# Masked attention of a Perceiver decoder: half of the softmax weights turned by VectorE blocks and device memory, weighing one place later, values copied by ScalarE

## The reference, cut to what matters

```python
Q = query @ Wq.T + bq ; K = key @ Wk.T + bk ; V = value @ Wv.T + bv      # 16 heads of 16
energy = einsum('bhqd,bhkd->bhqk', Q, K) / sqrt(16)
energy = where(mask == 0, -1e20, energy)
attention = softmax(energy, axis=-1)                                      # over 256 keys
x = einsum('bhqk,bhkd->bhqd', attention, V).reshape(b, -1, 256)
x = x @ Wo.T + bo
```

## Time and profile before

| | |
|---|---|
| median of three runs | 1993.7 us (1990.88 to 1994.27) |
| the profiled execution | 1994.13 us |
| its span | 1992.4 us |
| share of the span: PE, DVE, ACT, POOL | 98%, 62%, 56%, 30% |
| granted clock of TensorE | 0.996 |
| the 32 places of the masked attention | 981.4 to about 1250 us of the span |

### The profile page before, as it was taken

One profiled execution on the slowest core, in us unless ns is written; L12 is line 12 of the kernel. 1 busy time (PEld: TensorE's weight loads), 2 busy tenths in 40 slices (PEclk: granted clock), 3 DMA queues, 4 the chain that ended last, 5 costly groups with the idle time before them and its releaser, 6 DMA issues.

```text
span 1992.4 us, 43991 instructions
## 1 busy us (share of the span) xinstructions
PE 1944.6 (98%) x17307; PEld 1694.8 (85%) x17307; DVE 1231.6 (62%) x3579; ACT 1112.7 (56%) x2432; POOL 600.5 (30%) x652
## 2 busy tenths in 40 slices
PE   6999999999999998998999999999999999999998
PEld 5898998989998984777688887889999999999998
DVE  6767677776767665676588988438748623243212
ACT  5666666666667663332587877544444444444443
POOL 3111141111211101233122211444444444444444
PEclk9999999999999999999999999999999999999999
DMA  5556454555545441000311110001010010101000
GB/s 195 176 173 208 150 164 155 157 166 156 158 147 171 137 130 49 1 1 1 92 34 34 34 33 24 22 1 64 1 43 10 34 43 1 43 1 43 1 12 32
DMA packets 100332, 154.21 MB, mean 77 GB/s; under 512 B 12896, under 2 KB 78752, under 8 KB 100000
## 3 DMA queue, kind: packets, MB, share of 16 engines
q1 hardware_dynamic: 100128, 151.41, 24.4%
HBM read 103.73 MB, written 43.45 MB: 74 GB/s over the span
## 4 chain that ended last, share of the span: by engine, by line
PE 46%; ACT 2%; DVE 2%; issue 1%; POOL 0%; POOLq 0%; DVEq 0%; ACTq 0%
PE bank L83 21%; PE bank L1132 18%; PE bank L1053 2%; PE bank L1068 1%; PE bank L1040 1%; ACT att_p L1238 1%; PE bank L1098 1%; PE bank L1009 1%; ACT att_pt L1243 1%; PE bank L1079 0%; DVE dec_room L140 0%; POOL right_h L963 0%; ACT att_kt L1230 0%; PE bank L1091 0%; DVE att_vz L1385 0%
## 5 line engine op out<-in xcount | busy, mean ns | idle before, releaser
L963 POOL TENSOR_TENSOR right_h<-right_hr,right_h 128x512 fp32r<-128x512 f32 x256 | 341.7, 1335 | 417.6 <-ACT right_hr L1285 417.6
L1284 ACT ACTIVATE right_h<-bank,dec_b 128x512 fp32r<-128x512 f32 x256 | 176.2, 688 | 389.7 <-PE bank L83 368.0
L83 PE MATMUL bank<-lat_kv_t,lat_qk 128*128 128x320 f32 x1536 | 253.8, 314 | 1.7 <-DVE lat_qk L2456 1.7
L83 PE MATMUL bank<-lat_wv,lat_kv_t 128*128 128x512 f32 x960 | 243.3, 394 | 4.1 <-DVE lat_qk L2456 4.1
L83 PEld LDWEIGHTS bank<-lat_kv_t,lat_qk 128*128 128x128 f32 x1536 | 228.0, 188 | 14.6 <-DVE lat_qk L2456 5.3
L2320 ACT ACTIVATE lat_p<-bank,lat_neg_max 128x320 f32<-128x320 f32 x256 | 134.7, 527 | 146.5 <-DVE lat_neg_max L2461 146.5
L83 PEld LDWEIGHTS bank<-lat_wv,lat_kv_t 128*128 128x128 f32 x960 | 175.7, 189 | 34.9 <-DVE lat_qk L2456 4.5
L83 PE MATMUL bank<-dec_xt,dec_lo 128*128 128x512 f32 x512 | 200.5, 392 | 0.0
L2461 DVE TENSOR_REDUCE lat_neg_max<-bank 128x1 f32<-128x320 f32 x256 | 122.5, 485 | 95.3 <-PE bank L83 89.3
L1285 ACT ACTIVATE right_hr<-bank,dec_b 128x512 f32<-128x512 f32 x256 | 174.5, 682 | 0.0
L1132 PE MATMUL bank<-dec_hi,right_h 128*128 128x256 f32 x1024 | 161.6, 279 | 1.2 <-POOL right_h L963 1.2
(11 more groups left out here) (332 smaller groups left out, 3804.9 us busy)
## 6 DMA issues: line engine op xcount, KB each, us to landing
lat_turns<-lat_pb SPq DMA_DIRECT2D x63, 640.0 KB, 3.0
lat_pt<-lat_turns SPq DMA_DIRECT2D x252, 160.0 KB, 3.2
raw_w<-in_L_ffn_W SPq DMA_DIRECT2D x16, 1024.0 KB, 6.6
lat_ctx_raw<-in_ctx SPq DMA_DIRECT2D x16, 512.0 KB, 5.2
right_ctx_raw<-in_ctx_turned SPq DMA_DIRECT2D x16, 512.0 KB, 3.8
lat_kv_f<-in_ctx_turned SPq DMA_DIRECT2D x15, 512.0 KB, 4.4
lat_ctx_raw<-gate_rows SPq DMA_DIRECT2D x15, 512.0 KB, 4.8
lat_kv_t<-lat_lt SPq DMA_DIRECT2D x32, 128.0 KB, 4.5
```

What stands on the lines that cost most here:

```text
L83: mm = pe.matmul(out, lhs(a, k), rhs(b, k), start=first and k == 0 and n == 0, stop=last and k == KD - 1 and n == 2)
L963: pool.tensor_tensor(h[:, g % 2, 1, :], hr[:, g % 2, :], h[:, g % 2, 0, :].bitcast(F32), ALU.subtract).then_inc(h_lo, 1)
L1284: act.activation(h[:, n % 2, 0, :], h_bank[n % 2][:, :], ACT.Relu, bias=bias).then_inc(h_hi, 1)
```

## The change

1. Half m = 0 of places 0 to 30 is no longer turned by PE and ACT. DVE turns it in 32x32 blocks (`turn`, one transpose of 128x1024 from `p[0]` into `pb`), SP writes `pb` to device memory (`turns`, two buffers) and reads it back in four DMAs into `pt_early` (one buffer). `p[0]` now lies in place of the scores of that half (`sc[:, 0]`). Half m = 1, and both halves of place 31, are turned as before.
2. `weigh(b-1)` does both halves in one, as the last of PE's slot b, behind values_proj(b+1) and the side step. It waits for both ways of turning.
3. `normalise(b-1)` moves to the end of DVE's slot, behind `slot_late`.
4. The values are copied to `vz` (now three buffers) by ACT, without bias, out of `pt_bank[0]` (but for place 0). The bias of the values goes through `Wo` once: `output_bias` adds bv @ Wo to bo, as the weights of a row sum to one.
5. `project_output` moves ahead of keys_proj, into odd slots; side steps wait for the turn of the place before.
6. At the start, ACT's values_proj(0) stands ahead of its queries(0); it waits for POOL's fill of `vz`.

```diff
-            p = att.sb("p", [P, KD, R, S2])
-            pt = att.sb("pt", [P, KD, R, 2, P])
+            p_late = att.sb("p", [P, R, S2])
+            p = (sc[:, 0], p_late)
+            pb = att.sb("pb", [P, 4, R * 2, 32])
+            pt_early, pt_late = att.sb("pt_early", [P, 4, R, 2, 32]), att.sb("pt_late", [P, R, 2, P])
+            turns = nc.dram_tensor("att_turns", (2, P, R * S2), F32, kind="Internal").ap()
...
+            def weights_turned(b):                      # SP
+                sp.wait_ge(p_turned, b + 1)
+                wait(sp, pt_in[b % 2], 64 * (b // 2))
+                sp.dma_start(turns[b % 2], pb[:, :, :, :].rearrange("p g u c -> p (g u c)")).then_inc(p_out, 16)
+                sp.wait_ge(p_out, 16 * (b + 1))
+                wait(sp, o_psum, b)
+                for g in range(4):
+                    sp.dma_start(pt_early[g * 32:(g + 1) * 32].rearrange("p q r t c -> p q (r t c)"),
+                                 turns[b % 2].rearrange("(q p) (g c) -> g p q c", q=4, g=4)[g]).then_inc(pt_in[b % 2], 16)
...
-            for i in range(2, NT):
-                context(i)
+            context(2)
+            for b in range(B - 1):
+                weights_turned(b)
+                if b % 2 == 1 and (b + 5) // 2 < NT:
+                    context((b + 5) // 2)
...
             for b in range(B):                          # PE
                 energies(b)
+                if b == 0:
+                    output_bias()
                 if b >= 1:
                     turn(b - 1, 1)
+                if b >= 3 and b % 2 == 1:
+                    project_output((b - 3) // 2)
                 if b + 1 < B:
                     keys_proj(b + 1)
-                if b >= 1:
-                    weigh(b - 1, 0)
-                    weigh(b - 1, 1)
-                turn(b, 0)
-                if b + 1 < B:
                     values_proj(b + 1)
                 if b in in_slot:
-                    pe.wait_ge(pt_done, 4 * b + 2)
+                    pe.wait_ge(pt_done, 2 * b)
                     side_step(*in_slot[b])
-                if b >= 2 and b % 2 == 0:
-                    project_output(b // 2 - 1)
+                if b >= 1:
+                    weigh(b - 1)
             pe.wait_ge(s_low, 8 * B)
             hidden(0, 0)
+            turn(B - 1, 0)
             turn(B - 1, 1)
-            weigh(B - 1, 0)
-            weigh(B - 1, 1)
+            weigh(B - 1)
...
+            values_proj(0)                              # ACT, ahead of queries(0)
...
-                turn(b, 0)                              # ACT
                 for r in range(R):
+                    if b + 1 < B and r == 2:
+                        values_proj(b + 1)
                     weights_of(b, 1, r)
...
+            def turn(b):                                # DVE
+                dve.wait_ge(p_ready, 8 * b + 4)
+                wait(dve, p_out, 16 * b)
+                dve.transpose(pb[:, :, :, :], p[0].rearrange("p r (t g c) -> p g (r t) c", g=4, c=32)).then_inc(p_turned, 1)
...
             for b in range(B):                          # DVE
                 slot_head(b)
+                lowest(b, 0, 0, R)
                 if b >= 3 and b % 2 == 1:
                     residual(b // 2 - 1)
-                lowest(b, 0, 0, R)
                 lowest(b, 1, 0, R)
...
                 if b % 2 == 1:
                     add_bias(b // 2)
+                if b < B - 1:
+                    turn(b)
+                slot_early(b)
+                slot_late(b)
                 if b >= 1:
                     normalise(b - 1)
-                slot_early(b)
-                if b + 1 < B:
-                    values_proj(b + 1)
-                slot_late(b)
```

More of the change, by code:

```diff
@@ L890, in _ @@
                 sp.dma_start(mask_i[half * S:(half + 1) * S, :], w["mask_1x1xSxS2_ik1"]).then_inc(loads, 16)
-            for t in range(2):
-                sp.dma_start(bv[:, t, :], everywhere(w["L1_xattn_bv"])).then_inc(loads, 16)
+            with nc.allow_non_contiguous_dma(reason="a bias as a column"):
+                sp.dma_start(bv[:, :], column(w["L1_xattn_bv"])).then_inc(loads, 16)
             sp.dma_start(bo[:, :], everywhere(w["L1_xattn_bo"])).then_inc(loads, 16)
@@ L1236, in weights_of, with values_proj @@
                 if m == 1 and r == 0 and b >= 1:
[L1237 to L1238 removed]
+                    act.wait_ge(pt_psum, 2 * b)
+                act.activation(p[m][:, r, :], sc[:, m, r, :], ACT.Exp, bias=low[:, m, r:r + 1], scale=-1.0).then_inc(p_ready, 1)
             def turn(b, m):
+                u = turn_of(b, m)
                 for half in range(2):
[L1242 to L1244 removed]
+                    act.wait_ge(pt_psum, 2 * u + half + 1)
+                    own_r = slice(2 * half, 2 * half + 2)
+                    if m == 0:
+                        for n in range(2):
+                            ins = act.copy(pt_early[:, :, 2 * half + n, :, :],
+                                           pt_bank[half][:, n * 2 * P:(n + 1) * 2 * P].rearrange("p (t q c) -> p q t c", q=4, c=32))
+                        ins.then_inc(pt_done, 1)
+                    else:
+                        act.copy(pt_late[:, own_r].rearrange("p r t n -> p (r t n)"), pt_bank[half][:, :]).then_inc(pt_done, 1)
+            def values_proj(b):
+                act.wait_ge(v_psum, b + 1)
+                wait(act, o_psum, b - 2)
+                to = vz[:, b % 3].rearrange("p t m r e -> p (t m r e)").rearrange("p (u e) -> p u e", e=2 * W32)
+                src = values_bank(b)[:, :].rearrange("p (u h e) -> p u h e", h=2, e=HD)
+                for par in range(2):
+                    at = par * W32
+                    ins = act.copy(to[:, :, at:at + HD], src[:, :, par, :])
+                ins.then_inc(v_done, 1)
             def side_read(kind, c, j):
```

114 lines of the change are left out of this document (66 added, 48 removed).

## The result

| | kernel before | changed kernel |
|---|---|---|
| median | 1994.17 us (5 runs, 1990.88 to 1994.92) | 2002.61 us (5 runs, 2001.17 to 2006.62) |
| the profiled execution, its span | 1994.13, 1992.4 us | 2001.17, 1999.4 us |
| granted clock over the span | 0.996 | 0.993 |

The ratio is 1.0047, with a 95% interval of 1.0035 to 1.0059: the change makes the kernel slower by 0.47%. The prediction was 2000.5 us and slower, and its mechanism for the first ten places is the one that the trace shows. Two executions in the comparisons of this document, one of e3 and one of the kernel before beside c3, were slow ones at a low granted clock, and the ratios leave them out.

A forecast was written before the change was run, and what follows sets the result against it. PE was taken to bound the early places, with DVE nearly as full from place 10. Head +1.6, early +3.3, places 10 to 24 0, 25 to 30 -0.5, end +2.3 made +6.7: 2000.5 us, range 1987 to 2013.

The forecast's parts named there:

- the case itself: Whole kernel: the forecast of 2000.5 us, its own range 1998 to 2006, chance 0.42.
- The head: Start: PE's queries(1) comes later because ACT copies the values ahead of queries(0): +1.6 us, bounds 0 and +2.2.
- DVE's block turn: DVE, each place: transpose of 128x1024 takes 1.24 us, bounds 0.85 and 1.35; two early places 13.4 us, above PE's 12.82.
- The way: Block turn's end to last read's landing, through device memory: L = 7.6 us, bounds 6.7 and 8.6.
- The loop: Early places: normalise, lowest, turn, way and weighing hold two slots at 15.1 us; with filling the path, +3.3, bounds 0 and +7.
- Places 10 to 24: Later attention places, 130.46 us before: DVE's gain and the waits together 0, bounds -5 and +5.
- -5.1 and +5.1: Places 10 to 24: DVE's work if it never waits, -5.1 us, against waits of +1.3 and +3.8.
- three waits: Places 10 to 24, DVE: for the gates in slot 13, +1.3 us; for the experts' rows in slots 23 and 24, +3.8.
- Places 25 to 30: Six places like 17 to 22, DVE bound: -0.1 us each, -0.5 us.
- the charge of 3.8 us: Slots 23 and 24: normalise queues behind DVE's wait for ACT's copy of the experts' rows: +3.8 us for the two.
- The last place: Place 31: weigh(30) uncovered, turns before weigh(31); energies(31) to hidden(0, 1) 12.9 us against 10.53: +2.3, bounds +0.5 and +4.
- The values on ACT: ACT's copies, two places: 12.13 to 11.7 us, under PE's 12.82, so no term.

The follow-up runs named there:

- e3: Changed kernel with ACT's values_proj(0) behind queries(1) in the head: 1998.35 us, ratio 1.0028 to the kernel before.
- c3: Changed kernel with weighing behind the next place's energies, normalise, residual and project_output moved, two read buffers, queries first: 1990.74 us, ratio 0.9990 to the kernel before.
- e1: Changed kernel, weighing takes both halves from the one PE turned, so PE waits for no transfer; turn and transfers still run: 1991.86 us, ratio 0.9985.
- e4: Changed kernel with the early half written to device memory twice ahead of the reads: 2053.83 us, ratio 1.0302 to the kernel before.
- e8: As e1, with DVE's block turn and the transfers left out too: 1976.96 us, ratio 0.9915 to the kernel before.
- e9: Changed kernel with DVE's normalise ahead of the side work in places 23, 24 and 31: 2001.09 us, ratio 1.0048 to the kernel before.
- e2: Changed kernel with two buffers instead of one for the blocks read back: 2001.99 us, ratio 1.0038 to the kernel before.
- e11: Changed kernel with project_output behind keys_proj and residual behind lowest(b, 1): 1998.36 us, ratio 1.0026 to the kernel before.
- e6: Kernel before with only the values copied by ACT and their bias put through Wo once: 1993.11 us, ratio 0.9994 to the kernel before.
- e5: Changed kernel with PE's values_proj repeated, twice in place 1 and three times in place 3: 2003.39 us, ratio 1.0048 to the kernel before.
- c1: Changed kernel with two read buffers, queries first, values_proj repeated in places 1 and 3, project_output behind keys_proj: 1996.90 us, ratio 1.0019 to the kernel before.

## Why the prediction was right

Predicted 2000.5 (1998 to 2006 for the case itself), measured 2002.61: a growth of 6.8 us said, 8.4 found. The way through device memory in a loop that PE and DVE wait for is shown (e1, e4). That the number came so near is in part luck: the stage's terms were +1.6, +3.3, 0, -0.5 and +2.3, and the profiled execution has +1.6, +6.7, -2.4, +1.7 and +1.8, with -2.4 in stages that the change doesn't touch. Step by step:

**The head (+1.6).** As predicted: 20.49 against 18.9. ACT copies the values and only then the queries; PE's next query product waits for those:

```profile
965.85 0.65 ACT L1305 COPY att_vz<-bank 128x256 f32<-128x256 f32 x2 [4.42 <-PE bank L83]
966.38 1.46 ACT L1267 ACTIVATE q_bd<-bank,att_q_bias,att_q_scale 128x512 f32<-128x512 f32 x2
...
967.99 3.67 PE L1035 MATMUL bank<-rows_a,right_wq 128*128 128x512 f32 x8 [1.36 <-ACT q_bd L1267]
```

e3 undoes it.

**DVE's block turn (1.24 us).** All 31 in a view by tile (min, median, max in ns), the straight line through two smaller tiles was enough. What the step made of it was wrong: without the wait for the transfers two places take 13.11 us with DVE's turns (e1) and without them (e8), PE busy throughout, and not 13.4 with DVE as the bound.

```profile
L1446 DVE STREAM_TRANSPOSE att_pb<-att_sc x31: 1234/1237/1246, 986.2 to 1242.1; 128x1024 f32<-128x1024 f32 x31
```

**The way (L = 7.6 us).** 7.2 at its shortest (places 0 and 5), 7.7 on average over places 4 to 9, and 9.3 in place 2, beyond the upper bound of 8.6. e1 shows by its 10.8 us that it isn't hidden. The bound of 8.6 itself doesn't come out of the earlier trace rows: with their largest landing of the group, 3.8, the sum is 8.1. By the rule of the Trainium skill, "DMA: Bandwidth & Descriptors", section "Anatomy of one DMA", the way was 6.8, and the early places as fast as before. No place of the profiled execution came in that short.

**The loop (15.1 us for two places).** The steady part has it: energies(4) to (10) at 1014.14, 1030.12, 1045.36, 1060.20, so 15.98, 15.24, 14.84 us, 15.4 on average (the last is as short as two places were before). In place 6 DVE goes from normalise through `lowest` and split_keys to the block turn without standing still, and the way and the weighing follow, as the loop has it. Energies(2) was put at 996.5, and is at 996.47, which is luck: the turn ended 0.4 us and the way took 0.4 us less than said, and the weighing took 1.9 us in place of 1.1, at a granted clock of 0.50. What failed is the term's size: +3.3 predicted, +3.1 in e9's execution and +6.7 in the profiled one. The rest is what the first four places lose (32.9 us against 29.6 in e9) when a transfer comes late, as here (SP's queue, then the landings of all writes of the stage):

```profile
1003.02 0.34 SPq L937 DMA_DIRECT2D att_turns<-att_pb  x1
1007.86 2.12 SPq L941 DMA_DIRECT2D att_pt_early<-att_turns  x4
...
1014.31 1.73 SPq L941 DMA_DIRECT2D att_pt_early<-att_turns  x4
```

```profile
DMA to landing us min/median/max: 2.6/2.8/5.7
```

The reads at 1007.86 wait 4.8 us behind the write instead of 2.8, and those at 1014.31 for the weighing of place 2, which the same lateness had put off until then (the buffer is single). I had written that the single buffer adds nothing; in such a place it does, in the median of e2 it doesn't. The step's upper bound was too low by its own terms: with L at 8.6 they give +8, not +7.

**Places 10 to 24 (0).** -2.4 in the profiled execution, -0.9 in e9's, 0.0 in e3's. DVE is the fullest engine, as I said (118.7 of 128.0 us), though not without waits, and e8 and e4 both move the stretch: DVE's turn with the transfers, and the length of the way. That -5.1 and +5.1 cancelled was luck. The text names three waits and prices two, and neither of the two is seen in its place: place 13 takes 8.8 us (8.9 before), 23 and 24 together 16.8 (16.7). A wait that I hadn't priced is there instead, project_output's, 6.4 us in five places (e11).

**Places 25 to 30 (-0.5).** +1.7, the step that was wrong in sign. I had the charge of 3.8 us for the experts' rows in places 23 and 24, that is ahead of energies(25). A part of it falls in place 25, because PE must wait too: its turn's second bank is the one that DVE reads last.

```profile
1190.81 0.69 DVE L1561 TENSOR_TENSOR dec_xt<-bank,dec_xt 128x512 fp32r<-128x512 f32 x1 [0.95 <-ACT dec_xt L1322]
```

```profile
1191.65 0.63 PE L1086 MATMUL bank<-ident,att_p 128*128 128x128 f32 x4 [1.69 <-DVE dec_xt L1561]
1192.88 2.08 PE L1125 MATMUL bank<-att_wo,att_ot 128*128 128x256 f32 x4 [0.61 <-DVE att_ot L1474]
```

DVE's wait for ACT, 0.81 before, is 0.95; behind it PE waits 1.69 and then 0.61 for the normalised rows. Energies(25) to (26) is 12.1 us, 9.0 before. Place 27 grew more, 12.2 against 8.5, and place 29 has 11.5 against 9.8, with the experts' rows in neither: in place 27 PE waits 1.50 us for DVE's addition of the cell's result to x (L1553) and 1.39 for the normalised rows. Behind the waits of places 25 and 27 the granted clock is 0.50, as the two rows in the section on the result show, and PE's next two groups there, project_output and the keys, take 2.08 + 2.46 and 1.78 + 2.91 us, where they take 1.03 and 1.78 at full clock: about 3.6 us in all. I had no such term. In e11, with the wait ahead of project_output gone, the granted clock of places 25 to 30 is 1.00 and they take 54.9 us, 0.6 less than before the change, as I had said; in e1 and e2, at 0.91, they take 59.5 and 59.2. No run changes the clock alone there.

**The last place (+2.3).** +1.8. PE's rows:

```profile
1250.93 0.65 PE L1115 MATMUL bank<-att_pt_early,att_vz 128*32 128x64 f32 x32 [1.33 <-issue]
...
1253.46 1.04 PE L1086 MATMUL bank<-ident,att_sc 128*128 128x128 f32 x8
1254.84 1.23 PE L1086 MATMUL bank<-ident,att_p 128*128 128x128 f32 x8 [0.35 <-issue]
1256.74 0.65 PE L1115 MATMUL bank<-att_pt_early,att_vz 128*32 128x64 f32 x32 [0.68 <-ACT att_pt_late L1296]
```

Weigh(30) ends 6.5 us behind energies(31) (5.6 said), hidden(0, 0) takes 1.5 (2.6), turns and weighing 4.3 (4.7): 12.36 in place of 12.9, with two errors against each other.

**The values on ACT (no term).** e6: right, within what it can tell.

One reading of the rows was off and carried nothing: the chain's hundredths in the earlier trace rows add up to 51, not 52.

## What to carry to other kernels

A turn given to DVE and a transfer takes matmuls from PE, but puts a latency (here 7 to 8 us) into whatever loop it closes: write the loop down (normalise, lowest, turn, way, weighing), and compare its length with what PE needs before counting what PE saves. If the loop is longer, the gain needs an order in which the consumer stands behind the next producer, as in c3, which brought two places from 15.9 to 14.3 us, less than I had hoped. Ask then what the next engine has to spare: DVE was busy for 118 of 128 us of places 10 to 24. Look at every step that the new order moves ahead of what it depends on: project_output and normalise, moved with no thought of a wait, cost some 4 us.

## What I had not expected of the hardware

- The granted clock fell to 0.50 (1.2 GHz) for some 3 to 6 us of PE's work behind waits of 2.7 and 3.4 us, and for some 3 us behind pairs of shorter waits, 1.69 and 0.61 us (place 25), 1.50 and 1.39 (place 27); energies' weight loads took 1.37 us in place of 0.74. Keeping PE busy through the first two (e5) won nothing in the median.
- The kernels that turn through device memory spread more, whether PE waits for the way or not: 10.0 us in twelve runs of c1, 8.9 in eleven of e11, 8.6 in ten of e1, against 3.3 in 19, 4.7 in 12 and 6.6 in 23 of the kernel before. The same code's first ten places took 75.4 and 79.0 us. One profiled execution isn't enough to size a term of 3 us there.
- A write of 512 KB landed in 2.6 to 5.7 us, a read of 128 KB in 2.5 to 3.8; four reads took 1.73 to 2.94 us to issue.
